# Attention step: the product with the values in front of the transposes of the reciprocals, the copy of rT behind the second exponentials

## What is computed

```python
x = x + einsum('bct,bcd->bdt', x, w0[cond])            # layer 0: a 32x32 mix of the tokens
x = x + attention(x)                                   # layer 1
x = x + lora(x)                                        # layer 2: base weight and an adapter per sequence
x = x + einsum('bct,bcd->bdt', x, w3[subject])         # layer 3: a 32x32 mix of the tokens

def attention(x):   # 8 heads of 32 in 4 groups, window of 128 positions
    q, k, v = projections of x; q, k = rope(rms(q)), rope(rms(k))
    write k, v into the paged cache (blocks of 16), read the window back
    p = softmax(q k^T * SCALE, masked)                 # over the window and the own tokens
    o = p v
    return o Wo^T
```

## Time and profile before

| | |
|---|---|
| median of 3 runs | 305.37 us (302.78 to 307.06) |
| profiled execution, its own time | 302.65 us |
| its span, from the first to the last instruction | 300.8 us |
| mean granted TensorE clock | 0.905 |
| TensorE matmul busy | 210.8 us, 70% |
| VectorE busy | 209.0 us, 69% |
| GpSimd busy | 164.2 us, 55% |
| ScalarE busy | 131.8 us, 44% |

### The profile page before, as it was taken

The page is one execution under the profiler, slowest core; times in us unless marked ns, Lnnn a source line. Parts: engine busy times, 40 slices in busy tenths (PEclk is TensorE's granted clock), DMA queues, the critical chain, the costliest instruction groups (busy, mean ns, idle before and its releaser), DMA issues.

```text
span 300.8 us, 7985 instructions
## 1 busy us (share of the span) xinstructions
PE 210.8 (70%) x2402; PEld 155.9 (52%) x2402; DVE 209.0 (69%) x628; ACT 131.8 (44%) x491; POOL 164.2 (55%) x279
## 2 busy tenths in 40 slices
PE   0132599699899993005788876897868879988773
PEld 0112475455555551004667755675657667767641
DVE  0987947888699985204589876784884867878760
ACT  0220015155444553321756664465555744667510
POOL 4456856067555557754266666556656665673120
PEclk9999859799999998555799998997997998999998
DMA  5819995034611000023031434233424343331011
GB/s 151 258 34 209 211 381 112 17 107 136 194 55 46 29 20 35 32 64 97 4 111 55 118 89 129 73 110 93 142 58 113 95 128 74 115 104 58 20 37 35
DMA packets 18319, 29.70 MB, mean 99 GB/s; under 512 B 8189, under 2 KB 13640, under 8 KB 17906
## 3 DMA queue, kind: packets, MB, share of 16 engines
q0 software_dynamic: 7408, 19.04, 22.9%
q1 hardware_dynamic: 8130, 5.22, 6.0%
q10 hardware_dynamic: 2752, 5.08, 5.4%
HBM read 29.43 MB, written 7.34 MB: 122 GB/s over the span
## 4 chain that ended last, share of the span: by engine, by line
issue 28%; POOL 24%; PE 19%; DMA 16%; DVE 4%; POOLq 4%; ACT 3%; SPq 0%; ACTq 0%; DVEq 0%
DMA big<-in_pool,row_now 4%; DMA w0c<-in_w,w_i 4%; PE quad L1119 4%; POOL own L547 4%; PE quad L1171 4%; POOL big L482 3%; POOL work L504 3%; PE bank L1157 3%; POOL big L542 3%; DMA merged<-work,row_now 2%; POOLq L422 2%; POOL merged L517 2%; DMA big<-merged,row_now 2%; POOL w0c L436 2%; DMA con<-in_consts 2%
## 5 line engine op out<-in xcount | busy, mean ns | idle before, releaser
L699 ACT ACTIVATE work<-bank,nmx 128x164 f32<-128x164 f32 x128 | 49.6, 398 | 30.3 <-DVE nmx L981 24.7
L1157 PE MATMUL bank<-kt_rope,big 128*128 128x164 f32 x256 | 46.8, 319 | 0.0
L1157 PEld LDWEIGHTS bank<-kt_rope,big 128*128 128x128 f32 x256 | 43.4, 205 | 5.0 <-issue 0.8
L995 DVE TENSOR_TENSOR onT<-quad,rT 32x256 f32<-32x256 f32 x64 | 26.9, 420 | 21.9 <-PE quad L1171 20.4
L1153 PE MATMUL bank<-mask,identb 128*128 128x492 bf16 (+1 forms) x48 | 18.2, 379 | 30.3 <-DVE kt_rope L972 22.7
L981 DVE TENSOR_REDUCE nmx<-bank 128x3 f32<-128x492 f32 (+1 forms) x48 | 28.5, 593 | 12.3 <-PE bank L1157 12.1
L1119 PE MATMUL quad<-wqkv_sb,work 128*128 128x512 f32 x64 | 34.2, 660 | 2.8 <-ACT work L652 2.7
L988 DVE STREAM_TRANSPOSE work<-work 128x768 f32<-128x768 f32 (+2 forms) x96 | 34.7, 410 | 0.0
L682 ACT ACTIVATE big<-qT,con 128x256 f32<-128x256 f32 (+1 forms) x64 | 27.2, 512 | 0.1
L517 POOL DMA_INDIRECT merged<-work,row_now x16 | 18.3, 1141 | 15.4 <-ACT work L646 9.0
L436 POOL DMA_INDIRECT w0c<-in_w,w_i x16 | 16.9, 1054 | 17.9 <-DMA w0c<-in_w,w_i 7.1
(11 more groups left out here) (158 smaller groups left out, 469.6 us busy)
## 6 DMA issues: line engine op xcount, KB each, us to landing
merged<-big ACTq DMA_DIRECT2D x3, 1024.0 KB
xin<-in_x SPq DMA_DIRECT2D x16, 128.0 KB
out<-x4s SPq DMA_DIRECT2D x16, 128.0 KB, 2.0
w3bd<-in_w SPq DMA_DIRECT2D x64, 4.0 KB
con<-in_consts SPq DMA_DIRECT2D x1, 660.5 KB, 5.2
wqkv_sb<-in_wqkv ACTq DMA_DIRECT2D x1, 512.0 KB
wt_sb<-in_wt ACTq DMA_DIRECT2D x1, 256.0 KB
wp_sb<-in_wp ACTq DMA_DIRECT2D x1, 256.0 KB
```

The source lines that it names most:

```text
L699: act.activation(prob[:, p, hd, 0:NK], ps_sc[(p + i) % 2][:, j * NK:j * NK + NK], ACT.Exp, bias=nmx[:, p, hd:hd + 1], scale=1.0, accum_out ...
L995: ve.tensor_tensor(onT[rows, :, :].rearrange("p c (b n) -> p b c n", b=NB), ps_o[rows, :, 64 * (g % 2):64 * (g % 2) + 64].rearrange("p b ( ...
L1157: mm = pe.matmul(at[:, j * NK:j * NK + NK], qbd[:, p, hd, :], kT[:, p, hd // GSZ, 0:NK], start=False, stop=(j == n - 1), skip_group_check= ...
```

## The change

Two groups of instructions change places with their neighbours, one on TensorE and one on ScalarE. On TensorE `weighted` of t1 comes before the wait for `rwide` and the two transposes. On ScalarE the wait for the transposes and the copy to `rT` come after the exponentials of heads 3 to 5. No instruction is added or removed, and every semaphore counts as before.

```diff
@@ ScalarE, phase2 @@
                     exponents(0)
+                if valid(t):
+                    exponents(1)
                 if valid(t1):
                     act.wait_ge(rT_done, t1 + 1)
                     if not isinstance(t1, int) or t1 >= 1:
                         act.wait_ge(onT_done, G * t1)
                     act.copy(rT[:, :, :], ps_t.rearrange("p (c n) -> p c n", c=2)).then_inc(rT_copied, 1)
-                if valid(t):
-                    exponents(1)
                 tn, _, pn, _, _ = at_step4(h, u, -1)
                 if valid(tn) and reused(tn):
                     queries(tn, pn)
@@ TensorE, phase2 @@
                 if valid(t1):
                     if valid(t2):
                         pe.wait_ge(zs_done, t2 + 1)
+                    weighted(t1, p1, r1)
                     pe.wait_ge(rwide_done, 2 * (t1 + 1))
                     for c in range(2):
                         mm = pe.transpose(ps_t[:, 128 * c:128 * c + 128], rwide[:, 128 * c:128 * c + 128], ident)
                     mm.then_inc(rT_done, 1)
-                    weighted(t1, p1, r1)
```

## The result

The changed kernel took 306.8 us in the median of 20 runs (304.68 to 309.14), against 305.19 us (302.78 to 307.9) for the kernel before in 20 runs; ratio 1.0077, 95% interval 1.0048 to 1.0106. The forecast was 306.9 us in 302.5 to 310.5, within 2%. So the reorder costs 1.5 to 3.2 us (the interval of the ratio) and wins nothing. Some executions of a kernel came out over 1.5% longer than its fastest: medians here are of all runs, ratios only of the others. The profiled execution has a span of 303.7 us, 2.9 us more than before, at a mean granted clock of 0.906.

What follows compares the result with a forecast made beforehand. The prediction took GpSimd and its three gathers a step to bound the kernel from 164 to 263 us. Its terms summed to +1.5 us, added to the median of 305.37 us: 306.9 us, range 302.5 to 310.5.

Steps and rivals of the forecast that it cites:

- GpSimd's queue bounds the loop: Second phase, steps 4 to 11: GpSimd, issuing three gathers a step, sets the pace at 10.07 us a step.
- the hole is real: Loop: TensorE's 12.5 us wait for `rwide` sets the pace, so product first wins 13 us, giving 292 us; chance 0.05.
- The loop costs nothing under its cover: Steps 4 to 11: price 0, because `rden` lies ready 0.87 to 2.85 us before GpSimd asks for it.
- the serial part: Loop: transposes and copy of `rT` can delay VectorE's scaling by at most 0.41 + 0.37 = 0.8 us.
- step 9: Loop step making tile 9's scores: `rden` ended at 222.62 and `rwide` came 2.85 us later.
- Step 1: Before the loop, making tile 1's scores: transposes and copy of `rT` come between product and scaling; +0.6 us, ends 0 and 1.6.
- Steps 12 to 14: Written out after the loop: TensorE wins about 0.9 us, but VectorE's wait for tile 15's keys stops it; 0.
- Step 15: Written out: transposes moved behind the product fill no wait, so tile 15's scores come later; +0.4 us, ends 0 and 0.8.
- Step 16: Last product: the copy of `rT` with its signals comes onto the path before the scaling; +0.5 us, ends 0 and 0.8.
- The sum: All parts of the second phase: 0.6 + 0 + 0 + 0.4 + 0.5 = +1.5 us.
- The clock rival: Loop: TensorE falls to 1.2 GHz in each step, for some 6 us; +13 us, 318 us; chance 0.04.

Runs made afterwards that it cites:

- without the gather: Gather of the old cache left out of the second phase: in the kernel before 281.71 us, ratio 0.9279; in the changed kernel 287.64 us, ratio 0.9475.

## Why the prediction was right

- **GpSimd's queue bounds the loop.** Shown: the period stayed at 10.04 us, writing the loop out won 7.4 us, a shorter queue 22 us. The rival "the hole is real" is refuted: TensorE's wait fell by 8.1 us and nothing came of it.
- **The loop costs nothing under its cover.** Shown for the eight steps by the periods (10.04 and 10.06 us in two profiles with the new order in the loop, 10.07, 10.06 and 10.04 in three with ScalarE's half at most), and by the 0.4 us a step that appear when GpSimd is out of the way. I had bounded the serial part at 0.8 us; it measured half of that. The cover itself was 0.87 to 3.04 us: I had taken step 9 (2.85) for the longest, and step 5 is longer.
- **Step 1, +0.6 us.** Not shown. The mechanism is there: VectorE's scaling waits for `rT` (1.37 us, at 154.32). But from the first `rwide` to the second the profiles before and after have 8.88 and 9.12 us, +0.24 only, and the other profiles say that this time follows something else. With the old order in that step it was 8.51, 8.02, 8.26 and 7.94 us (ScalarE's half, new order in the loop, written out, without the gather), with the new one 8.76, 8.01 and 7.94 (new order at the edges, written out, without the gather). The four of them with the same clock, 0.66 from 144 to 149 us, are 8.02 and 7.94 in the old order and 8.01 and 7.94 in the new: no difference. The profile before, from which I took the term, has this clock too, but its product took 2.9 us from 149.32, with a pause of 0.31 us in which the engine waited for nothing shown; the changed kernel's took 2.05. I had carried the slow product over.
- **Steps 12 to 14, gain held by the keys of tile 15.** Right: VectorE waited 1.97 us there, 0.75 before.
- **Step 15, +0.4 us.** +0.43 (from +1.87 at the keys of tile 15 to +2.30 at the maximum). The time from the `rwide` of step 15 to that of step 16 repeats it: 7.76, 7.81 and 7.82 us with the old order there (before, ScalarE's half, written out), 8.18, 8.19 and 8.20 with the new one (after, new order at the edges, written out).
- **Step 16, +0.5 us.** +0.60, and the scaling names ScalarE's `rT` as what it waited for. It starts 2.51 us after 290.35, where the product now stands in the place of the transposes; I had said some 2.5. From the last `rwide` to the end the same six profiles have 13.53 to 13.57 us and 14.14 to 14.19.
- **The sum** was +1.5 us, and the runs say 1.5 to 3.2 us. From the `rwide` of step 12 to the end these profiles have 45.59, 45.79 and 45.70 us in the old order and 46.74, 47.01 and 47.59 in the new: 1.15 to 1.9 us, where my terms were 0.9. So the cost lies in the last steps, they cost somewhat more than I had priced, and step 1 less. That the two errors cancel, and that the forecast met the median to 0.1 us, is luck. The new order in the loop alone measured +0.5% with unchanged periods, so something beside my terms may be in it.
- **The clock rival.** It did not come: the mean granted clock over the eight steps is 0.98, against 0.92 before. But this isn't the change's doing. ScalarE's half alone, in which TensorE waits for `rwide` no less than before, has 0.98 too (TensorE's wait and the clock from 176 to 256 us), and the new order at the edges, with the old one in the loop, has 0.96:

```profile
PE bank L1204 <- POOL rwide L563: 13.8, 7, 2.5
```

```profile
176.00:256.00 80.00, 60.72 (x1031) 49.25 (x1030) 57.04 (x151) 44.63 (x177) 48.40 (x96) 0.98 0.35 101
```

I had tied a fall to waits of 2.1 to 2.6 us. ScalarE's half alone has five waits of 2.08 to 2.53 us in the loop: one was followed by a fall (0.83 from 185 to 195 us), four by none (1.00 in each later stretch of 10 us to 255). What decides it stays open. The Trainium skill (TensorE: Matmul & The Clock Gate, Part 1) has idle time as what leaves the engine throttled; the trace agrees where the order changed back, 3.31 us of idle time being followed by 0.50. The idle stretch that is left in front of the transposes I had estimated at 2.0 us; it was 1.1 at most, because TensorE now also waits about 1 us a step for the queries.

## What to carry to other kernels

A wait that heads the list is worth something only if the instruction it delays is on the path. Ask how long the input of the late engine had been ready: here `rden` had lain there for 0.87 to 3.04 us, and a hole of 12.5 us closed to 4.4 for no gain. And before a producer is moved behind independent work, see what stood behind its consumer in an in-order queue: one 0.37 us copy, left in front of the exponentials, turned a 2 us loss into one of 14 us. A cover found in the profile holds until the covering engine is made faster; a reorder that is free today then costs 0.4 us a step.

## What the runs showed that I had not expected

The pace of eight equal steps was set by GpSimd so firmly that it was 10.04 to 10.07 us in five kernels, while the clock of TensorE over the same steps lay between 0.92 and 0.98. The same statements in a loop cost GpSimd more than written out: 10.07 against 8.82 us a step once the gather's landing was out of the way as well. The instructions are about as long in both; the loop has gaps between them that the written-out step lacks or has shorter, for instance 0.43 us in front of `rwide` and 0.38 us in front of the row numbers of the old cache's gather. What fills these gaps no trace here shows.
